# A slot of eight whole image rows: one 12 KB run per partition, projection steps of four slots

## What is computed

```python
def reference(x, conv1_w, conv1_b, convl_w, convl_b, conv2_w, conv2_b, H_w, H_b):
    return x + conv(gn(x))            # gn: 32 groups of 24 channels, over pixels and channels
# conv:
    xc = conv2d(x, conv1_w, conv1_b)                 # 1x1: 768 -> 16 channels
    h = mean(xc, pixels) @ H_w.T + H_b               # 4 experts, the best two, softmax
    g = softmax(where(top2(h), h, -inf))
    for i in range(4):                               # 3x3 conv at 1, 2, 4, 8 times the size
        f = 2 ** i
        experts.append(resize(conv2d(resize(xc, f), convl_w, convl_b), 1 / f))
    out = conv2d(sum(g[i] * experts[i]), conv2_w, conv2_b)   # 1x1: 16 -> 768 channels
```

## Time and profile before

| | |
|---|---|
| timed runs | 1449.02, 1452.35, 1459.64 us |
| median | 1452.35 us |
| profiled execution, its span | 1451.0 us |
| instructions in it | 24,055 |

### The profile page before, as it was taken

How to read it: one execution, slowest core, us unless ns; L and a number is a source line. 1 busy time by engine, 2 the same in 40 slices (tenths; PEclk the granted TensorE clock), 3 DMA queues, 4 the chain that set the end, 5 groups by cost and what they waited for, 6 DMA issues and landing times.

```text
span 1451.0 us, 24055 instructions
## 1 busy us (share of the span) xinstructions
PE 1189.7 (82%) x8700; PEld 814.9 (56%) x8700; DVE 1029.3 (71%) x2747; ACT 661.9 (46%) x1549; POOL 313.9 (22%) x381
## 2 busy tenths in 40 slices
PE   0679999988987999789968899887787899779863
PEld 0466676656654777466546666555555665445531
DVE  6869988678469897764797884569766755636654
ACT  3578999553423797545225784411551352100110
POOL 1083003403041000340540001065004104344100
PEclk9989999999986999799978999978898898667865
DMA  9798897499999999999999998999999999999999
GB/s 344 256 359 318 301 370 288 176 392 319 399 366 416 409 389 349 378 395 387 392 412 411 390 377 288 388 396 402 416 390 344 399 411 414 417 416 410 401 416 388
DMA packets 188162, 540.01 MB, mean 372 GB/s; under 512 B 12810, under 2 KB 12810, under 8 KB 188044
## 3 DMA queue, kind: packets, MB, share of 16 engines
q1 hardware_dynamic: 118140, 336.75, 61.4%
q10 hardware_dynamic: 69904, 201.74, 34.9%
HBM read 337.12 MB, written 201.33 MB: 371 GB/s over the span
## 4 chain that ended last, share of the span: by engine, by line
PE 45%; DMA 23%; DVE 16%; ACT 5%; issue 5%; SPq 4%; POOL 1%; ACTq 0%; DVEq 0%; POOLq 0%
PE ring_ps L680 16%; DMA x_sb<-in_x 12%; DMA out<-x_sb 10%; PE conv_ps L750 10%; DVE x_sb L1010 9%; PE img_ps L697 8%; PE ring_ps L781 8%; DVE stats L926 7%; SPq L521 3%; ACT xT L803 2%; PE ring_ps L710 1%; SPq L494 1%; PE ring_ps L769 1%; ACT unread_squares L831 1%; ACT unread_copy L833 1%
## 5 line engine op out<-in xcount | busy, mean ns | idle before, releaser
L1010 DVE TENSOR_TENSOR x_sb<-x_sb,ring_ps 128x768 f32<-128x768 f32 x512 | 462.1, 950 | 299.5 <-PE ring_ps L781 215.8
L926 DVE BATCH_NORM_STATS2 stats<-x_sb 128x6 f32<-128x192 f32 x1792 | 473.0, 344 | 36.7 <-DMA x_sb<-in_x 26.8
L803 ACT COPY xT<-ring_ps 128x1024 f32<-128x1024 f32 x384 | 377.0, 1012 | 194.1 <-PE ring_ps L680 130.7
L781 PE MATMUL ring_ps<-w,es 128*128 128x512 f32 (+1 forms) x1024 | 335.8, 447 | 126.0 <-DVE x_sb L1010 107.7
L680 PE MATMUL ring_ps<-ident,x_sb 128*128 128x128 f32 x3072 | 402.4, 284 | 25.2 <-DVE x_sb L1010 10.4
L680 PEld LDWEIGHTS ring_ps<-ident,x_sb 128*128 128x128 f32 x3072 | 351.5, 146 | 101.9 <-issue 56.0
L781 PEld LDWEIGHTS ring_ps<-w,es 128*128 128x128 f32 x1024 | 190.9, 232 | 250.1 <-DVE x_sb L1010 169.2
L643 POOL TENSOR_TENSOR band<-taps,masks 128x640 f32<-128x640 f32 (+1 forms) x112 | 132.9, 1203 | 515.7 <-PE conv_ps L750 511.9
L697 PE MATMUL img_ps<-xT,w 128*32 128x256 f32 x3072 | 216.2, 389 | 16.2 <-ACT xT L803 15.2
L750 PE MATMUL conv_ps<-xc,band 128*128 128x1 f32 (+8 forms) x1120 | 221.4, 346 | 0.7 <-POOL band L643 0.7
L750 PEld LDWEIGHTS conv_ps<-xc,band 128*128 128x128 f32 x1120 | 159.0, 198 | 69.9 <-issue 67.3
(11 more groups left out here) (94 smaller groups left out, 361.1 us busy)
## 6 DMA issues: line engine op xcount, KB each, us to landing
x_sb<-in_x SPq DMA_DIRECT2D x128, 1536.0 KB, 11.3
out<-x_sb ACTq DMA_DIRECT2D x256, 768.0 KB, 9.8
x_sb<-in_x SPq DMA_DIRECT2D x172, 768.0 KB, 9.3
w_rep<-in_L_conv_conv_w ACTq DMA_DIRECT2D x1, 384.0 KB
wl_raw<-in_L_conv_convl_w SPq DMA_DIRECT2D x8, 9.0 KB
gate_w<-in_L_conv_H_w SPq DMA_DIRECT2D x8, 0.2 KB
w_raw<-in_L_conv_conv_w SPq DMA_DIRECT2D x1, 48.0 KB
b_raw<-in_L_conv_conv_b SPq DMA_DIRECT2D x2, 3.0 KB
```

The costliest lines, as they stand in the source:

```text
L781: last = nc.tensor.matmul(flat_ps[:, buf, part], es4[:, q, (i % 4) * P:(i % 4 + 1) * P], w2[:, part], start=True, stop=True)
L803: nc.scalar.copy(xT[:, at % XT], ring_ps[:, TURN["T", a, n] % RING]).then_inc(xT_copied, 1)
L926: ins = nc.vector.bn_stats(stats[:, c, g, :], group)
L1010: nc.vector.tensor_tensor(x_sb[:, n, 2 * half + q % 2, :], x_sb[:, n, 2 * half + q % 2, :], flat_ps[:, TURN["E", b, t] % RING, 0:D], ALU.a ...
```

## The change

A slot becomes eight whole image rows. A sample's rows are split as (j t r): slot i = 4 t + j holds the rows 16 j + 8 t to 16 j + 8 t + 7; the 64 columns are split as (w q), so that a partition holds four neighbouring pixels of a row. A slot is then one contiguous piece of memory, 12 KB per partition, and half a slot 6 KB per partition.

A projection step still takes 128 channels and eight transposes, but now from four slots and two of the four pixel columns: steps 0 to 11 read slots 4 to 7, steps 12 to 23 slots 0 to 3. So a load into a slot given away waits for step 11 or step 23 of its last tenant (line 517), and TensorE waits for four slots at steps 0 and 12. So that the image keeps its order of pixels for the convolution, the image copy writes with a step of four elements, and the high and the low half read the convolution's result so. An expansion tile takes its quarter from the other index of `es4`, and the waits between tiles and the copies to `es4` follow. `TRANSFERS`, `KEPT` and the three order lists are as before.

```diff
-    slots_of = "b (q p j bb) w c -> b p j (bb w) q c"
-    x_v = x.rearrange(slots_of, q=QN, p=2, j=4, bb=2)
-    out_v = out.rearrange(slots_of, q=QN, p=2, j=4, bb=2)
+    slots_of = "b (j t r) (w q) c -> b t j (r w) q c"
+    x_v = x.rearrange(slots_of, j=4, t=2, r=NB, q=QN)
+    out_v = out.rearrange(slots_of, j=4, t=2, r=NB, q=QN)
...
-        def pair(s, c):
-
-            (n0, k0, _), (n1, k1, _) = loads["L", s, 2 * c], loads["L", s, 2 * c + 1]
-            return (loaded[n0], 16 * k0), (loaded[n1], 16 * k1), n0[0], n1[0]
+        def quad(s, t):
+
+            at = [loads["L", s, 4 * t + j][:2] for j in range(4)]
+            return [(loaded[n], 16 * k) for n, k in at]
...
-                            sp.wait_ge(transposed, AI[s0] * STEPS + (CHUNKS - i0 // 2) * KB)
+                            sp.wait_ge(transposed, AI[s0] * STEPS + (2 - i0 // 4) * 2 * KB)
...
-                if k == 0:
-                    for ready in pair(a, c)[:2]:
+                if k == 0 and c % 2:
+                    for ready in quad(a, c // 2):
                         pe.wait_ge(*ready)
                 buf = bank_free(("T", a, n))
-                for q in range(QN):
-                    for half in range(2):
+                for j in range(4):
+                    for h in range(2):
                         last = nc.tensor.transpose(
-                            ring_ps[:, buf, q, half * P:(half + 1) * P],
-                            slot("L", a, 2 * c + half)[:, q, k * P:(k + 1) * P], ident[:, :])
+                            ring_ps[:, buf, j, h * P:(h + 1) * P],
+                            slot("L", a, 4 * (c // 2) + j)[:, 2 * (c % 2) + h, k * P:(k + 1) * P], ident[:, :])
...
-                if i % 4 == 0:
-                    pe.wait_ge(es4_ready, BI[b] * 4 + 2 * (i // 4) + q // 2 + 1)
+                if i % 2 == 0 and q == 0:
+                    pe.wait_ge(es4_ready, BI[b] * 4 + i // 2 + 1)
...
-                    last = nc.tensor.matmul(flat_ps[:, buf, part], es4[:, q, (i % 4) * P:(i % 4 + 1) * P], w2[:, part],
+                    last = nc.tensor.matmul(flat_ps[:, buf, part], es4[:, i % 4, q * P:(q + 1) * P], w2[:, part],
...
-                nc.scalar.activation(xc[:, XC_PLACE[a], :], img_ps[:, :], ACT.Identity,
+                nc.scalar.activation(xc[:, XC_PLACE[a], :].rearrange("p (x q) -> p q x", q=QN),
+                                     img_ps[:, :].rearrange("p (q x) -> p q x", q=QN), ACT.Identity,
...
-                nc.scalar.activation(es_hi[:, :], conv_ps[:, :], ACT.Identity, bias=bias_es[:, b:b + 1]
+                nc.scalar.activation(es_hi[:, :].rearrange("p (q x) -> p q x", q=QN),
+                                     conv_ps[:, :].rearrange("p (x q) -> p q x", q=QN), ACT.Identity, bias=bias_es[:, b:b + 1]
...
-                    act.wait_ge(expanded, BI[b] * TILES + 3 * QN + 2 * half + 2)
+                    act.wait_ge(expanded, BI[b] * TILES + (2 * half + 2) * QN)
                 elif BI[b]:
-                    act.wait_ge(expanded, (BI[b] - 1) * TILES + 7 * QN + 2 * half + 2)
+                    act.wait_ge(expanded, (BI[b] - 1) * TILES + (2 * half + 6) * QN)
...
-                nc.vector.scalar_tensor_tensor(es_lo[:, :], conv_ps[:, :], bias_es[:, b:b + 1],
-                                               es_hi[:, :].bitcast(F32), ALU.add, ALU.subtract).then_inc(lo_ready, 1)
+                by_column = "p (q x) -> p q x"
+                nc.vector.scalar_tensor_tensor(es_lo[:, :].rearrange(by_column, q=QN),
+                                               conv_ps[:, :].rearrange("p (x q) -> p q x", q=QN), bias_es[:, b:b + 1],
+                                               es_hi[:, :].bitcast(F32).rearrange(by_column, q=QN), ALU.add, ALU.subtract).then_inc(lo_ready, 1)
```

More of the change, by code:

```diff
@@ L695, in project @@
                 pe.wait_ge(xT_copied, at + 1)
-                for q in range(QN):
+                for j in range(4):
                     last = nc.tensor.matmul(
-                        img_ps[32 * q:32 * q + 32, 2 * P * (c % 2):2 * P * (c % 2 + 1)],
-                        w1[:, AI[a] % 2, k, R * (1 - c // 2):R * (3 - c // 2)], xT[:, at % XT, q, :], start=(n == 0), stop=(n == STEPS - 1))
+                        img_ps[32 * j:32 * j + 32, 2 * P * (c % 2):2 * P * (c % 2 + 1)],
+                        w1[:, AI[a] % 2, k, R * (1 - c // 2):R * (3 - c // 2)], xT[:, at % XT, j, :], start=(n == 0), stop=(n == STEPS - 1))
                 last.then_inc(projected, 1)
```

## The result

The changed kernel takes 1530.93 us in the median of four runs (1527.60 to 1533.95), the kernel before 1451.69 beside it: a ratio of 1.0536 (95% interval 1.0503 to 1.0569), 79 us slower. The prediction said slower, 1483 us within 1444 to 1516: the sign came, the size was missed by 48 us, outside the range. The profiled execution of after has a span of 1532.0 us; all rows of after are from it.

The account below looks back on a forecast made before the run. Engines were taken to set the pace in the loading stages (100 to 250, 490 to 600 us), DMA in most of the rest. 1451 + 51 (holds) - 20 (longer runs) + 1.35 (median) = 1483 us, range 1444 to 1516.

Parts of the forecast that it names:

- The bound and the mechanism: Engines pace the loading stages, DMA most of the rest; slots freed in fours delay loads there by some 10 us.
- The chain for the first stage: Late loads delay statistics of samples 8, 3, 2 to 170.6, 221.6, 266.8 us; sample 8's square root to 190.2.
- The stretched holds: 47 transfers wait for a later step: 25 us for the first 23, 26 for 24 later, sum 51 us.
- rival B: Only the first loading stage is lost, later holds being covered by queued transfers: 1457 us, chance 0.20.
- 75 if ScalarE's in-order waits spread: Upper end for the cost of the later slot releases: 75 us instead of 51.
- Longer runs: 103,936 fewer packets save 26.6 us of DMA time; 76% of bytes move where DMA is the bound: 20 us gained.
- the gap between one and two queues: Packet time at 402 against 416 GB/s, 122.3 and 118.2 ns: 4.1 ns taken as a packet's cost beyond its bytes.
- Arithmetic: Counts and shapes stay; stepped access in image copy, high and low half costs nothing, 36 us of engine time if doubled.
- The expansion's waits for its copies: TensorE's matmuls wait 10.4 us in 12 waits for weight copies; change taken as nothing, at most 10 us gain.
- A: DMA-bound stretches run at the saturated rate throughout with cheaper packets, 80 us less: 1423 us, chance 0.12.
- C: A long run costs as much per byte as four short ones, so no gain: 1503 us, chance 0.13.
- The signs named beforehand: Packets about 84,200, saturated rate 420 GB/s or more, lower GB/s in 100 to 250 us, half as many transpose waits.

Follow-up runs that it names:

- e6: Kernel before with the later slot release only for the 23 transfers whose slot's last tenant is one of the first seven samples: 1491.40 us, ratio 1.0248.
- e3: Changed kernel with the square roots of samples 8, 9 and 2 ahead of the next sample's first statistics in ScalarE's list: 1534.12 us, ratio 1.0563.
- e1: Kernel before with only the later release, loads waiting for step 11 or 23, layout and 3 KB runs as before: 1550.79 us, ratio 1.068.
- e15: Kernel before with the later slot release only for the 24 later transfers, the first 23 released in pairs as before: 1521.11 us, ratio 1.0461.
- e5: Changed kernel with those square roots first and 81 groups of ScalarE's statistics moved behind the step that frees their slot: 1515.09 us, ratio 1.0421.
- e9: Changed kernel with eight reloads moved ahead of loads that wait for a later step, in SP's list: 1527.05 us, ratio 1.0495.
- e11: Changed kernel with the reload moves of e9 and two more, so four reloads precede two waiting loads of sample 1: 1530.19 us, ratio 1.0533.
- e2: Kernel before with only the longer runs of 12 and 6 KB, releases as before, pixels in wrong places of the image: 1440.35 us, ratio 0.9923.
- e12: Kernel before with 12 KB runs and slots still freed in pairs, four image quarters outermost in a transfer: 5298.09 us, ratio 3.648.
- e13: As e12, with 32 pixel groups outermost and quarters inside, so products read every fourth column: 1626.39 us, ratio 1.1186.

## Why the prediction was right and wrong

**The bound and the mechanism: right.** The loading stages wait for slots, and slots that come free in fours starve them. The bursts are there, SP's issues of after, of the loads after step 11 and after step 23 of sample 4:

```profile
156.36 2.66 SPq L521 DMA_DIRECT2D x_sb<-in_x  x4
...
181.66 2.04 SPq L521 DMA_DIRECT2D x_sb<-in_x  x4
```

(In the earlier trace rows two leave at 145.26 and two at 156.25.) The chain for the first stage was near in every member. VectorE's last statistics of sample 8, then 3, then 2, after (the answers cut the last two off at their end; the start counts):

```profile
170.57 7.36 DVE L928 BATCH_NORM_STATS2 stats<-x_sb 128x6 f32<-128x192 f32 x28
...
223.46 2.69 DVE L928 BATCH_NORM_STATS2 stats<-x_sb 128x6 f32<-128x192 f32 x10
...
270.72 4.51 DVE L928 BATCH_NORM_STATS2 stats<-x_sb 128x6 f32<-128x192 f32 x17 [0.62 <-DMA x_sb<-in_x]
```

Predicted were 170.6, 221.6 and 266.8, and 190.2 for the square root, which came at 190.15. Some of this nearness is luck: the chain counted no gain from longer runs, which after has, and with the holds alone (e6) the three starts are 175.28, 228.22 and 274.90, 5 to 8 us after the forecast. One link had the right number for a wrong reason: the projections of sample 8 are 15.1 late not through the square root but through the copy behind the same statistics (e3).

**The stretched holds, 51 us: mis-sized; this is the step that failed.** They cost 98 (e1), and the 47 us between are nearly all of the 48 missed. The first 23 were put at 25 and cost 38 alone (e6), some 31 in after. The later 24 were put at 26, "at the same price", and cost 67 alone (e15). That price was a mean over a stage in which the first six held transfers cost little (at sample 4's first projection after is 0.1 us late, e6 4.0); the next twelve, up to sample 2's, cost 24 us in both, 2.0 each. From sample 13 on nearly every loading sample lost 6 to 15 us (e15). TensorE was busy 107.1 of 110 us there before; the prediction quoted that row against rival B and did not draw the price from it. That this fullness makes the later holds dearer is argued, not tried. The prediction had "75 if ScalarE's in-order waits spread" as an upper end. They did spread (e5 gives 16 us back), and the sum still lies above that end. How the rest divides between the loads' own lateness and what stands behind it in the lists isn't settled; the order of reloads isn't part of it (e9 to e11).

**Longer runs, -20 us: near as a sum, by luck, with both factors wrong.** The saving in DMA time was 46 us in e2 for 26.6, that is 7.1 ns a packet (46 x 16 / 103,936) and not the 4.1 of the gap between one and two queues. But 12 of it reached the end, 27% and not 76%: the stretches with a DMA share of 0.99 and 1.01 did not get shorter by what their packets saved. One reading is a loop, in which each reload waits for a store, that for an addition, and so on: SP's waits for stores at L524 are 663.0 us in e2 for 670.5. The other is that the packets' time overstates the room, as the rate of two full queues says (some 18 us). No run parts the two. In after the step from e1 is 20; why a held kernel gains more than e2 isn't settled. The Trainium skill (DMA: Bandwidth & Descriptors, Where 436 GB/s comes from) has HBM bind at about 358 GB/s per core; the 424 of one queue in after speak against it here again.

**Arithmetic, nothing: right but for one group.** The rows of the image copy, the low and the high half in after:

```profile
L841 ACT ACTIVATE xc<-img_ps,bias 128x512 f32<-128x512 f32 x16 | 18.9, 1184 | 6.6 <-PE img_ps L697 6.5
L1003 DVE SCALAR_TENSOR_TENSOR es_lo<-conv_ps,bias_es,es_hi 128x512 fp32r<-128x512 f32 x16 | 11.9, 746 | 20.2 <-ACT es_hi L856 20.2
L856 ACT ACTIVATE es_hi<-conv_ps,bias_es 128x512 fp32r<-128x512 f32 x16 | 11.0, 688 | 156.6 <-PE conv_ps L750 118.8 <-DVE x_sb L1014 37.8
```

The image copy before:

```profile
L841 ACT ACTIVATE xc<-img_ps,bias 128x512 f32<-128x512 f32 x16 | 11.0, 685 | 6.0 <-PE img_ps L697 5.9
```

The two that read with a step take what they took (747 ns for the low half in the earlier trace rows, 687 for the high half before). The image copy, which writes with one, takes 1184 ns for 685: 16 x 0.5 = 8 us of ScalarE, of which no run shows what reaches the end. The row it was priced by was one that reads. The expansion's waits for its copies, put at nothing, went from 10.4 us to 9.2 in 11 waits.

**The rivals.** A, DMA-bound stretches at the saturated rate: no, 370 and 378 GB/s after, and 380 in e2 without holds. B, only the first stage is lost: no (e15). C, long runs no cheaper: no (e2). The signs named beforehand came: packets 84,226, the saturated rate 421 and 424, 281 GB/s in 100 to 250 us, fewer and longer waits of SP (33 for 53, where half as many were named). Sound signs of the mechanism don't vouch for the size: none of them priced a hold after the first stage.

## What to carry to other kernels

Here the unit in which a buffer comes free was worth more than the length of a run: 98 us lost against 12 to 20 gained. When a wait is stretched in many places, price it stage by stage from the row of that stage, and not by the mean of the first one, whose first holds cost little here; ask there what in each in-order list stands behind the instruction that will wait. Before crediting cheaper transfers to a stretch with a full DMA share, look for a loop of store, reload and addition that would keep its pace; the gain by the full rate (some 18 us here) came nearer to the 12 measured than the packets' time did.

## What the runs showed of the hardware

- The outermost dimension of a transfer's access set how many DMA engines it used: with 4 entries outermost (e12) the share was 0.25, that of 4 engines in 16, and the rate 102 GB/s on average, with 32 (e13) and the same bytes 333. The Trainium skill (DMA: Bandwidth & Descriptors, Rules for kernel authors) states this rule, and the trace agrees.
- Access with a step of four float32 elements: free in reading PSUM on ScalarE (688 ns for 687, and 1013 for 1012) and VectorE (746 for 747); dear in writing SBUF on ScalarE (1184 for 685, 1979 for 1006) and in what a product streams on TensorE (628 for 389, mean granted clock 0.88 in both runs). Writing with a step of 256 elements cost as much (1977 for 1012).
- Packets of 6 and 12 KB instead of 3 KB saved 46 us of the packets' time in 1397, some 3%, and raised the full rate of one queue from 402 to 424 GB/s, of two from 416 to 421 and 424.
